# Layer-1 attention on eight cores: the row of block 0 first in every head pair, and quantisation two steps behind the norm

## The reference, cut to what matters

```python
q, k, v = proj(Wq, bq), proj(Wk, bk), proj(Wv, bv)      # 16 heads of 64, blocks of 64 tokens
row_scores = gq @ k * scale                             # blocks 0 and 63 of n=4096 (here 0 and 31 of 2048):
out_rows = softmax(row_scores) @ v                      #   every key
local = softmax(qb @ [k(n-1), k(n), k(n+1)]) @ v        # all blocks: three neighbouring blocks
glob = softmax(qb @ k[global blocks]) @ v               #   plus the global blocks, own softmax
final = local + glob; final[global blocks] = out_rows
x = x + final @ Wo.T + bo
h = bit_linear(layernorm(x), w1)                        # activations rounded to 127 / max|row|
```

## Time and profile before

| | us |
|---|---|
| median of 3 runs | 2241.38 |
| the three runs | 2239.27, 2241.38, 2412.34 |
| the profiled execution | 2243.92 |
| its span, slowest core (core 0) | 2242.0 |
| spans of the eight cores | 2222.3 to 2242.0 |

### The profile page before, as it was taken

How to read it: one execution, slowest core, us unless ns; L and a number is a source line. 1 busy time by engine, 2 the same in 40 slices (tenths; PEclk the granted TensorE clock), 3 DMA queues, 4 the chain that set the end, 5 groups by cost and what they waited for, 6 DMA issues and landing times. The chain is left out here.

```text
span 2242.0 us, 35450 instructions; the slowest of 8 cores (2222.3 to 2242.0 us)
## 1 busy us (share of the span) xinstructions
PE 1936.3 (86%) x12314; PEld 902.4 (40%) x12314; DVE 1181.6 (53%) x2085; ACT 1102.9 (49%) x2049; POOL 94.3 (4%) x152
## 2 busy tenths in 40 slices
PE   4899899977899995999988888777786799969999
PEld 3443334322344442444434444444333344434444
DVE  4234656455355422414637666665475588875442
ACT  5577777646211000111217777777564488863331
POOL 0000000000000000000000000000343000000000
PEclk9899999988899997999999999788797899979999
DMA  7203564200587307640002000100200422241332
GB/s 186 40 1 121 172 183 146 48 1 1 109 232 232 123 2 158 172 71 2 1 1 39 6 6 11 39 11 2 38 1 1 142 76 76 76 132 60 114 118 84
DMA packets 65035, 170.13 MB, mean 76 GB/s; under 512 B 4448, under 2 KB 37216, under 8 KB 57696
## 3 DMA queue, kind: packets, MB, share of 16 engines
q1 hardware_dynamic: 58352, 134.31, 18.5%
q0 software_dynamic: 6512, 33.56, 9.0%
HBM read 167.85 MB, written 33.55 MB: 90 GB/s over the span
## 5 line engine op out<-in xcount | busy, mean ns | idle before, releaser
L637 PE MATMUL f0R<-lnT,wgu 128*128 128x512 bf16 x1536 | 336.0, 382 | 27.4 <-DMA wgu<-f0wgu_d 27.4
L396 ACT ACTIVATE a0bq<-a0S 128x1024 bf16<-128x1024 f32 (+1 forms) x320 | 268.6, 893 | 119.2 <-PE a0S L316 118.5
L672 ACT ACTIVATE f0si<-f0R 128x1024 bf16<-128x1024 f32 x48 | 49.2, 1024 | 387.2 <-PE f0R L637 387.2
L637 PEld LDWEIGHTS f0R<-lnT,wgu 128*128 128x128 bf16 x1536 | 151.4, 99 | 211.8 <-issue 33.4
L1363 PE MATMUL g1hp<-q1T,t 128*128 128x512 bf16 x1024 | 226.1, 382 | 7.1 <-DVE g1a L1442 5.5
L1387 PE MATMUL g1hp<-g1t,q1T 128*128 128x512 fp8e4 x1024 | 222.9, 381 | 1.8 <-ACT q1T L1421 1.8
L698 DVE TENSOR_TENSOR f0hT<-f0si,f0R 128x1024 bf16<-128x1024 bf16 x48 | 58.6, 1221 | 226.5 <-PE f0R L637 226.5
L1125 ACT ACTIVATE a1pt<-a1T 128x768 bf16<-128x768 bf16 (+2 forms) x152 | 118.5, 784 | 83.2 <-PE a1T L1005 69.5
L1363 PEld LDWEIGHTS g1hp<-q1T,t 128*128 128x128 fp8e4 x1024 | 98.7, 98 | 134.3 <-issue 21.9
L1387 PEld LDWEIGHTS g1hp<-g1t,q1T 128*128 128x128 bf16 x1024 | 100.6, 98 | 123.8 <-issue 4.3
L938 PE MATMUL a1pj<-lnT,wqk 128*128 128x512 bf16 x512 | 143.3, 433 | 4.2 <-POOLq L881 4.2
(11 more groups left out here) (195 smaller groups left out, 2995.0 us busy)
## 6 DMA issues: line engine op xcount, KB each, us to landing
a0wst<-g1w_d SPq DMA_DIRECT2D x64, 512.0 KB, 4.8
f0wst<-g1w_d SPq DMA_DIRECT2D x32, 1024.0 KB, 6.3
hs_scr<-g1hsp SPq DMA_DIRECT2D x32, 512.0 KB, 3.2
q1T<-hs_scr SPq DMA_DIRECT2D x8, 2048.0 KB, 9.0
wgu<-f0wgu_d POOLq DMA_DIRECT2D x24, 512.0 KB, 7.0
xs<-x SPq DMA_DIRECT2D x8, 1024.0 KB, 11.8
t_scr<-f0wt SPq DMA_DIRECT2D x32, 256.0 KB, 2.5
xo<-xs SPq DMA_DIRECT2D x16, 512.0 KB, 8.9
```

Of the source, the lines that this page charges most:

```text
L396: s.activation(bq[:, u % 4, :, n0:512], sS[:, u % 2, :, n0:512], AF.Square).then_inc(s_sq, 1)
L637: mm = t.matmul(R[:, k % 4, 512 * n2:512 * (n2 + 1)], wgu[:, cc % 3, x, j, :], lnT[:, j, t0 + 512 * n2:t0 + 512 * (n2 + 1)], start=(j == 0 ...
```

## The change

1. Items of a head pair run in the order 16, 0, 1, ..., 15: the row of block 0 is first. The waits on the last projections of a pair (`last_qk`, the last q, for pair 0 the last v) move from S of tile 0 to S of the row. Counters (`item`, `use`, `tile_of_use`) follow.
2. Fills: `due = (i % 17 * n + 15) // 16`, so none at the row, all by the iteration of tile 15 (with 12 fills the pattern is three iterations with a fill and one without, starting with tile 0; with 8 fills every second iteration, starting with tile 0).
3. Pair 7: the row's X is on VectorE like in the other pairs (L902 is gone); tiles are finished in the order 0, 1, ..., 15; `finish(k)` runs from the iteration of tile 4 on, through the three draining iterations too, for k = 0 to 14, and `finish(15)` alone comes after.
4. `finish(k)` is now Z(k-2), W, W, Q(k-3), N(k), and `lx` has three buffers, the third at 8 KB. The list ends Q13, Z14, Q14, Z15, Q15.
5. That buffer lies where chunks 8 to 11 of `t1` were: the early load takes 8 chunks, the load at the start of the next stage 24, and TensorE waits for the second load at chunk 8 and not at 12.

```diff
     def finish(k):
-        if k >= 1:
-            out.append(("Z", k - 1, done[k - 1]))
-        out.extend([("W", done[k], 0), ("W", done[k], 1)])
         if k >= 2:
-            out.append(("Q", k - 2, done[k - 2]))
-        out.append(("N", k, done[k]))
+            out.append(("Z", k - 2))
+        out.extend([("W", k, 0), ("W", k, 1)])
+        if k >= 3:
+            out.append(("Q", k - 3))
+        out.append(("N", k))
...
-    items = [(p, m) for p in range(8) for m in range(17)]
+    items = [(p, (m + 16) % 17) for p in range(8) for m in range(17)]
...
-            due = n if m == 16 else (m * (n - 2) + 14) // 15
+            due = (i % 17 * n + 15) // 16
             while n - len(fill) < due:
                 out.append(fill.pop(0))
-        elif i < len(items) and m >= 5:
-            finish(m - 5)
-    for k in range(12, NT):
-        finish(k)
-    return out + [("Q", 14, done[14]), ("Z", 15, done[15]), ("Q", 15, done[15])]
+        elif i >= 7 * 17 + 5:
+            finish(i - 7 * 17 - 5)
+    finish(NT - 1)
+    return out + [("Q", 13), ("Z", 14), ("Q", 14), ("Z", 15), ("Q", 15)]
...
-        lx = [place(nc, p + f"lx{i}", 120 - 8 * i, [128, D], F32) for i in range(2)]
+        lx = [place(nc, p + f"lx{i}", kb, [128, D], F32) for i, kb in enumerate((120, 112, 8))]
...
-                    if it[0] == "X" and it[1] == 7:                      # GpSimd
+                    if it[0] == "X" and it[1] == 7 and it[2] < 16:
...
-                sp.wait_ge(s_av, use(4, 0))
-                sp.dma_start(t1[:, 0:12, :, :], ...)
+                sp.wait_ge(s_av, use(4, 16))
+                sp.dma_start(t1[:, 0:8, :, :], ...)
...
                     elif it[0] == "S":                                   # TensorE, the row
-                        t.wait_ge(s_x, item(pr, 16))
+                        pj_out(t, last_qk[pr])
+                        pj_out(t, banked[("P", "q", pr, 3)])
+                        if pr == 0:
+                            pj_out(t, last_v[0])
+                        if pr >= 1:
+                            t.wait_ge(s_x, item(pr, 16))
...
-                        if k >= 2:                                       # ScalarE, N
-                            s.wait_ge(N.ap, k - 1)
-                        s.activation(lx[k % 2][:, :], ...)
+                        if k >= 3:
+                            s.wait_ge(N.ap, k - 2)
+                        s.activation(lx[k % 3][:, :], ...)
...
-                sp.dma_start(t1[:, 12:32, :, :], ...)                    # next stage
+                sp.dma_start(t1[:, 8:32, :, :], ...)
...
-                    if c in (0, 12):
-                        t.wait_ge(l_t1[c // 12], 16)
+                    if c in (0, 8):
+                        t.wait_ge(l_t1[c // 8], 16)
```

More of the change, by code:

```diff
@@ L743, in a1_order @@
     out = []
-    done = list(range(1, NT)) + [0]
     def finish(k):
-        if k >= 1:
-            out.append(("Z", k - 1, done[k - 1]))
-        out.extend([("W", done[k], 0), ("W", done[k], 1)])
         if k >= 2:
-            out.append(("Q", k - 2, done[k - 2]))
-        out.append(("N", k, done[k]))
+            out.append(("Z", k - 2))
[3 more added lines that the diff above has]
+        out.append(("N", k))
     for c in range(4):
@@ L760, in a1_order @@
             p, m = items[i]
-            if m == 0:
+            if m == 16:
                 fill = []
@@ L812, in item @@
     def item(pr, m):
-        return 17 * pr + m
+        return 17 * pr + (m + 1) % 17
     def use(pr, m, k=0):
-        return 19 * pr + m + k
+        return 19 * pr + (k if m == 16 else m + 3)
     def tile_of_use(b):
         pr, r = b // 19, b % 19
-        return (pr, r, 0) if r < 16 else (pr, 16, r - 16)
+        return (pr, 16, r) if r < 3 else (pr, r - 3, 0)
     with contextlib.ExitStack() as es:
@@ L890, in _ @@
                 for it in order:
[L891 removed]
+                    if it[0] == "X" and it[1] == 7 and it[2] < 16:
                         m = it[2]
                         g.wait_ge(s_rr, m + 1)
[L894 to L902 removed]
+                        for u in range(1 if m == 0 else 0, 2):
+                            lo = 64 if u == 0 else 0
+                            g.tensor_scalar(pp[:, m % 2, u, lo:lo + 192], pp[:, m % 2, u, lo:lo + 192],
+                                            rr[:, m % 2, 0, u:u + 1], None, ALU.mult)
+                            x = g.tensor_scalar(pp[:, m % 2, u, 256:384], pp[:, m % 2, u, 256:384],
+                                                rr[:, m % 2, 1, u:u + 1], None, ALU.mult)
                         x.then_inc(s_p7, 1)
                     elif it[0] == "Z":
[L905 removed]
+                        k = ti = it[1]
                         g.wait_ge(s_qz, k + 1)
@@ L944, in _ @@
                         if m == 0:
[L945 to L951 removed]
+                            t.wait_ge(s_x, item(pr, 0))
+                        else:
                             t.wait_ge(s_x, item(pr, m) - 1)
@@ L992, in _ @@
                         b = use(pr, m, k)
-                        if pr == 7:
+                        if pr == 7 and m < 16:
                             t.wait_ge(s_p7, m + 1)
@@ L1187, in _ @@
                                         negate=True).then_inc(s_mx, 1)
-                    elif it[0] == "X" and it[1] == 7:
+                    elif it[0] == "X" and it[1] == 7 and it[2] < 16:
                         _, pr, m = it
                         v.wait_ge(s_x, item(pr, m) + 1)
-                        if 2 <= m < 16:
+                        if m >= 2:
                             v.wait_ge(s_p7, m - 1)
-                        if m < 16:
-                            u0 = 1 if m == 0 else 0
-                            v.reciprocal(rr[:, m % 2, :, u0:2], den[:, m % 2, :, u0:2]).then_inc(s_rr, 1)
-                        else:
-                            v.reciprocal(rr[:, 2, 0, 0:1], den[:, 2, 0, 0:1]).then_inc(s_rr, 1)
+                        u0 = 1 if m == 0 else 0
+                        v.reciprocal(rr[:, m % 2, :, u0:2], den[:, m % 2, :, u0:2]).then_inc(s_rr, 1)
                     elif it[0] == "X":
```

40 lines of the change are left out of this document (11 added, 29 removed).

## The result

| us | before | after |
|---|---|---|
| median of the runs | 2241.8 (17 runs) | 2213.3 (4 runs) |
| ratio after/before, 95% interval | | 0.9869 [0.9835, 0.9903] |
| the profiled execution | 2243.92 | 2209.91 |
| its span, slowest core | 2242.0 (core 0) | 2208.2 (core 4) |

The changed kernel takes some 29 us less, 1.3%: within 2%, and inside the range, but 8 us above the forecast of 2205.

The account below looks back on a forecast made before the run. VectorE was taken to bound pair 7's step with 6.53 us of its own work, no engine being full in the head pairs. +3.7 - 3.8 - 34.3 - 2.1 = -36.5 from 2241.4 gave 2205, range 2191 to 2228.

Parts of the forecast that it names:

- The step: Pair 7's finishing steps: VectorE's 1.59 us hole before Z goes, 8.12 falls to 6.6 with items, 6.0 without; -34.3 us.
- The end: Last W to the next stage: the last residual add no longer stands behind a Z; -2.1 us.
- First W one iteration earlier: Pair 7: the first W comes after tile 4's scores, not tile 5's; 3.78 us earlier.
- The row's stretch: Row's scores to the next tile's: 5.8 to 6.3 us in every pair, the bare chain being 5.80.
- The extra row in front of pair 7's tiles: Eight rows instead of seven precede pair 7's tiles; the added chain, placed in pair 0, costs +5.80 us.
- Pairs 4 to 6: Row's stretch -3.3, tile 15's iteration -1.6, fill in tile 0's iteration +1.0: -3.9 us each, -11.7 for three.
- Pairs 0 to 3: Two fills move from the row's stretch to tile iterations: +1.2 us a pair, bounds 0 and 7.2; +4.8 for four.
- the 4.8 for the transposes: One more set of row transposes and A before pair 7's tiles: its iteration takes 5.84 against 1.00, +4.8 us.
- VectorE held by GpSimd: Rival: in each step the rounding waits for GpSimd's scaling, at most 0.75 us; 15 steps, +11, 2216; 15%.
- The step doesn't shrink: Rival: a loop hidden by the hole keeps pair 7's step at 8.12 us; only -12, 2230; 8%.
- More than 2% faster: Rival: pairs 4 to 6 keep the high clock, the four before lose nothing, early steps cost no more; 2194; 13%.
- The clock: Rival: fills fall to half clock after TensorE idles, up to 1.7 us each; slower from 22 more; 2266 if half fell; 6%.

Follow-up runs that it names:

- x1: Kernel before the change with only Z two steps behind and the third buffer, row still last: 2216.8 us, ratio 0.9894.
- x3: Changed kernel with no fill in tile 0's iteration, fills from tile 1 on: 2208.1 us, ratio 0.9879.
- z3: Changed kernel plus sixteen 128x512 matmuls that nobody reads in the row's iteration of pairs 0 to 6: 2201.6 us, ratio 0.9816.
- y1: Changed kernel; pairs 0 to 3: two fills beside the row, none in tile 0's iteration; pairs 4 to 6: one beside the row; 2211.5 us, ratio 0.9827.
- v1: y1's fills in pairs 0 to 3, changed kernel's in 4 to 6 plus sixteen useless matmuls beside the row, more around last two Q: 2193.4 us, ratio 0.9798.
- w1: y1 plus useless matmuls in the row's iteration of pairs 4 to 7, pair 7's tiles 0 to 3 and around the last two Q: 2205.0 us, ratio 0.9825.

## Why the prediction was right and where it was not

**The step, right.** Z's wait for `lx` was the one hole, it is gone, and VectorE bounds. Forecast 6.6 with items and 6.0 without; measured 6.46 to 6.51 in the steady steps (the first is 7.3, and on some cores the third is some 8.05) and 5.55 to 6.14 without items. VectorE's own work of 6.53 was the number to take, and nothing was to be added to it. Fifteen steps of core 4 from the first W (1610.58) to the last (1707.04) are 96.5 us, forecast 99.1. x1 shows that the lag alone gives this.

**The end, right.** The last W to the next stage 16.30, forecast 18.83 - 2.1 = 16.7.

**First W one iteration earlier, right.** -3.4 by the means, forecast -3.8.

**The row's stretch, nearly right.** Forecast 5.8 to 6.3 in every pair; the means over the cores are 5.8 to 6.2 but in pair 5, which has 6.5, and single cores reach 6.7. The extra row in front of pair 7's tiles costs 5.8, as forecast. The 5.80 and 9.49 that the forecast took for the stretch before were one core's: the means before are 6.4 to 6.7 in pairs 0 to 3 and 8.6 to 9.0 in pairs 4 to 6. With nothing that could shorten the chain maximum to exponential, the idle time of TensorE in it is the price of every row.

**Pairs 4 to 6, right in the sum, and in part by luck.** -10.9 by the means, forecast -11.7. It is not -3.9 in each, though: -6.5, -4.4 and 0.0. The row's stretch gives -2.7 a pair (forecast -3.3) and tile 15's iteration -1.6, as forecast. Pair 6, from whose border the terms were taken, has both, but loses 4.1 us in its tiles 2 to 14. The fills that ran at least partly at the low clock go with it: 3.5, 4.4 and 3.2 in pairs 4, 5 and 6 before, 1.0, 2.0 and 3.4 after. The terms of the forecast have no such part.

**Pairs 0 to 3, wrong: the failing step is the price of the fill in tile 0's iteration.** The text took +1.2 a pair, 0.6 of it for the filled pattern and so 0.6 for this fill, from bounds of 0 and 7.2, and stayed "near the lower end since in rows 2 a fill costs next to nothing". Measured: +8.6 in pair 0, which is +3.8 if the 4.8 for the transposes holds, and +2.7, +2.4 and +3.0 in the next three: +3.0 in the mean in place of +1.2. The text had seen the half clock (3.59 against 1.89) but priced it by fills in the middle of a pair, where an iteration waits anyway for ScalarE and VectorE and hides the fill. Tile 0's iteration had been 0.99 long: nothing waits there, and a fill of 3.59 in it lies bare. By the means of pairs 1 to 3 tile 0's iteration is 3.9 us longer, of which tile 1's gives 1.7 back: 2.25 in place of 0.6. The other tiles cost 1.1 in place of 0.6, and the row's stretch gives 0.6 back. The rows to price the fill by were the border's own, not the earlier trace rows. Over pairs 0 to 3 the loss is 11.9 us. x3 (a place where the fill is hidden, still at the low clock) leaves 2.1 of it, z3 (same place, full clock) 2.8, and y1 (the row covered with real fills) none, it is 1.7 below: they show both halves of the price.

**The account.** Forecast -0.1 - 36.4 = -36.5; measured +8.3 - 39.0 = -30.7 in the stage, and -29 in the runs. The fills in pairs 0 to 3 are 2.6 + 4.5 = 7.1 of the 8.4 us lost before the first W; the 2.6 won behind it and 1.2 in the next stage take part of that back. The measured time lies in the range, and even in the forecast's own 2196 to 2214, though only just; that the miss stayed so small is partly luck, in pairs 4 to 6 and in the 2.6 and 1.2.

**The rivals.** *VectorE held by GpSimd*: false. The rounding takes 0.80 beside GpSimd's scaling, 0.75 alone, so 0.05 a step and not 0.75; it is GpSimd's instruction, the one that started first, that is stretched (0.77 to 1.16), as in the earlier trace rows. The Trainium skill ("SBUF — State Buffer", section "SBUF: two separate sides") says of a VectorE instruction in a 2-port mode and one of GpSimd that the later of the two fully blocks. If the rounding is such an instruction, which no run shows by itself, this isn't borne out here. *The step doesn't shrink*: false. *More than 2% faster*: not this kernel, but its conditions are what v1 makes (no loss in pairs 0 to 3, pairs 4 to 6 kept): 2193.4, where 2194 was worked out. v1 adds work that this rival did not have, and its first step is not shorter (8.8 on core 0), so that the two numbers agree so closely is partly chance. *The clock*: true in its kind behind the row, where the forecast lost 7 us, but not as it was counted. It needed 22 more fills at the low level than before. On a core 18 to 22 of the 72 ran at least partly at that level before and 13 to 18 after: 8.1 and 10.2 in pairs 0 to 3, 11.1 and 6.4 in pairs 4 to 6 (means). So there were fewer, not more, and the loss in pairs 0 to 3 comes less from their number than from where they lie: tile 0's iteration had no fill before.

**Still open.** Why eight fills in a pattern other than every second iteration cost 4 us in pair 4 (x3), why pair 6 gains nothing in after, and why eight useless matmuls beside the row made pairs 4 to 6 slower in w1 (0.7 to 1.5 us each, against y1), when sixteen made the three together 2.8 us faster in z3 (against after, whose fills lie otherwise than y1's). None was tried apart.

## What to carry to other kernels

- Where one engine waits in each step for what another made in the same step, put a step between them in the list and pay a buffer: it brought 1.6 us a step here, and the forecast is the bound engine's own work, with nothing added.
- Work that moves out of a stretch bounded by a chain of other engines leaves TensorE idle there, and what comes first behind the gap pays twice: at the low clock, and in an iteration that hid nothing. Price a moved instruction by the iteration that it lands in, not by the mean of its kind.
- Put real work into such a gap, up to the length of the chain, and keep the iteration behind it free; where there is none, matmuls that nobody reads pay, but in w1 most such places gave nothing, so each is to be tried.

## What the runs showed of the hardware that was not expected

- 29 us of matmuls without use took 11.7 us off the time from the first scores to the first W (z3 against after), and 10.5 off the stage.
- Eight 128x512 matmuls take 3.59 us behind a TensorE idle time of 4.01 (granted clock 0.50), and 1.90 where the idle time was filled (1.00). The first 64 of the next stage take 16.58 behind idle times of 4.95 and 1.58 (after, core 4), and 13.97 on every core of w1 and v1, where most of these were filled.
- A low clock can cost next to nothing: in x3 tile 0's and tile 1's iterations ran wholly at the low level and were 2.6 us shorter than in after, since the fill stood where the iteration waits anyway.
- The slow GpSimd scaling of the row, 5.44 us with TensorE idle for 7.44 until its end, was worth 1.8 us when it took 0.75: ScalarE stood right behind it, at 4.97. What ends an idle time last says little of what ends it next.
